# The transpose of the convolved x: four TensorE transposes a step, or VectorE 32x32 squares placed by DMA through memory

## What is computed

```
gate, xBC, dt = split(h @ in_proj_w.T)            # 8192, 8192 + 2*8*128, 128
xBC = silu(causal_conv4(xBC) + conv_b)
x, B, C = split(xBC)                              # 128 heads of 64; 8 groups of B and C
scores = (C @ B.T) * tril(exp(cs_l - cs_s))       # per head, chunks of 128 tokens, states carried over
y = scores @ (x * dt) + x * D                     # x * dt with tokens down the partitions
yg = y * silu(gate)
out = rmsnorm_per_group(yg) * norm_w @ out_proj_w.T
```

## Time and profile before

| what | us |
|---|---|
| median of 3 executions (1624.51 to 1627.74) | 1625.1 |
| the profiled execution's own time | 1627.01 |
| its span in the trace | 1625.2 |
| PE busy | 1564.3 (96%) |
| DVE busy | 1228.0 (76%) |
| POOL busy | 1052.0 (65%) |
| ACT busy | 1002.3 (62%) |
| mean DMA rate | 81 GB/s |

### The profile page before, as it was taken

The page is one execution under the profiler, slowest core; times in us unless marked ns, Lnnn a source line. Parts: engine busy times, 40 slices in busy tenths (PEclk is TensorE's granted clock), DMA queues, the critical chain, the costliest instruction groups (busy, mean ns, idle before and its releaser), DMA issues. The chain is left out here.

```text
span 1625.2 us, 25474 instructions
## 1 busy us (share of the span) xinstructions
PE 1564.3 (96%) x8296; PEld 1226.0 (75%) x8296; DVE 1228.0 (76%) x1689; ACT 1002.3 (62%) x2122; POOL 1052.0 (65%) x790
## 2 busy tenths in 40 slices
PE   6979999999999999999999999999999999999979
PEld 4657777777777777777777777777777777777757
DVE  6688877787778877887688877887688877887565
ACT  4357765666666665666666665666666665666431
POOL 2017874788757874788657874787657874787620
PEclk9899999999999999999999999999999999999989
DMA  3033321323222221222212321223222221322011
GB/s 118 1 103 103 107 91 59 92 91 92 78 72 92 92 92 59 91 92 92 78 72 92 92 91 59 92 92 92 78 75 88 92 92 59 98 86 84 20 40 53
DMA packets 73658, 131.65 MB, mean 81 GB/s; under 512 B 10944, under 2 KB 10944, under 8 KB 73280
## 3 DMA queue, kind: packets, MB, share of 16 engines
q1 hardware_dynamic: 73536, 130.09, 24.3%
HBM read 127.44 MB, written 2.62 MB: 80 GB/s over the span
## 5 line engine op out<-in xcount | busy, mean ns | idle before, releaser
L892 DVE SCALAR_TENSOR_TENSOR mx_acc<-bank,mx_cw,mx_acc 128x510 f32<-128x510 f32 (+2 forms) x480 | 358.3, 746 | 160.8 <-ACT mx_acc L877 149.5
L159 PE MATMUL bank<-h_hi,mx_w_hi 128*128 128x512 f32 x1152 | 465.6, 404 | 4.4 <-DVE mx_acc L892 2.3
L161 PE MATMUL bank<-h_hi,mx_w_lo 128*128 128x512 f32 x1152 | 453.1, 393 | 0.0
L160 PE MATMUL bank<-h_lo,mx_w_hi 128*128 128x512 f32 x1152 | 450.2, 391 | 0.0
L1108 ACT ACTIVATE mx_mix<-mx_csb,mx_gncs 128x256 f32<-128x256 f32 x512 | 218.9, 499 | 284.3 <-PE bank L1478 281.3
L1033 POOL TENSOR_TENSOR mx_y<-mx_y,mx_sg 128x512 f32<-128x512 f32 x128 | 338.4, 2644 | 59.7 <-DVE mx_y L1280 51.7
L839 POOL TENSOR_TENSOR mx_w_lo<-mx_w_raw,mx_w_hi 128x512 fp32r<-128x512 f32 x144 | 187.4, 1302 | 111.0 <-ACT mx_w_hi L834 111.0
L161 PEld LDWEIGHTS bank<-h_hi,mx_w_lo 128*128 128x128 f32 x1152 | 216.9, 188 | 48.5
L159 PEld LDWEIGHTS bank<-h_hi,mx_w_hi 128*128 128x128 f32 x1152 | 217.3, 189 | 47.8 <-issue 6.5
L160 PEld LDWEIGHTS bank<-h_lo,mx_w_hi 128*128 128x128 f32 x1152 | 217.7, 189 | 41.5
L1262 DVE TENSOR_TENSOR mx_mix<-mx_mix,mx_cbt 128x1536 f32<-128x1536 f32 x128 | 224.5, 1754 | 0.0
(11 more groups left out here) (163 smaller groups left out, 2203.7 us busy)
## 6 DMA issues: line engine op xcount, KB each, us to landing
mx_csb<-cs_rows SPq DMA_DIRECT2D x128, 512.0 KB, 4.0
mx_w_raw<-in_w_in SPq DMA_DIRECT2D x144, 256.0 KB, 4.0
mx_wo_raw<-in_w_out SPq DMA_DIRECT2D x64, 256.0 KB, 4.2
res<-in_x SPq DMA_DIRECT2D x8, 256.0 KB, 5.0
f_base_raw<-in_base_wt SPq DMA_DIRECT2D x2, 1024.0 KB, 6.1
out<-res SPq DMA_DIRECT2D x8, 256.0 KB, 2.0
f_a_raw<-in_lora_a SPq DMA_DIRECT2D x2, 256.0 KB, 3.8
f_lb_raw<-in_lora_b SPq DMA_DIRECT2D x2, 256.0 KB, 6.2
```

What stands on the lines that cost most here:

```text
L159: nc.tensor.matmul(out, w_hi, x_hi, start=first, stop=False)
L160: nc.tensor.matmul(out, w_hi, x_lo, start=False, stop=False)
L161: return nc.tensor.matmul(out, w_lo, x_hi, start=False, stop=last)
L892: self.nc.vector.scalar_tensor_tensor(dst, src[:, :, 0:SEQ - k], self.cw[:, c, TAPS - 1 - k:TAPS - k], dst, ALU.mult, ALU.add).then_inc(s[ ...
```

## The change

TensorE no longer transposes x. After `silu_conv` of unit `st + 4`, VectorE transposes that unit in 32x32 squares (`turn_squares`) into the slot of `th` whose tanh it has just used, laid out so that the squares of one 128x128 block lie row by row. SyncE (`move_x`) writes the slot to `x_dram` in memory and waits for that write, then loads it back with four DMAs, one for each 32 partitions of `xt`, in runs of 128 elements (512 bytes); all four count on `x_in`. `scale_x` reads `xt` instead of T_BANK and stands behind the taps of the step, `silu_conv` ahead of `silu_gate`, `turn_squares` of the next step's x behind `silu_gate`. `gdt` is laid out anew and made by four instructions a group instead of one. The copy `gncs` is gone: ScalarE reads the whole `ncs`. `square` writes into the gate's slot `sg` (the buffer `sq` is gone), and `tanh_gate` waits for the sums that read it. T_BANK, now S_BANK, holds the sums of squares alone. SyncE's groups are written out, not looped.

```diff
+            def move_x(g, st):
+                i, u = st % 2, st + 4
+                sp.wait_ge(s["turned"], 1 + STEPS * g + st + 1)
+                if not (first(g) and st < 2):
+                    x_moved(sp, *((g, st - 2) if st >= 2 else (g - 1, st + STEPS - 2)))
+                sp.dma_start(x_dram[i, :, :], th[:, u % 2, :]).then_inc(x_out[i], 16)
+                step_slot_freed(sp, s["xd"], g, st)
+                sp.wait_ge(x_out[i], 16 * (XT * g + st // 2 + 1))
+                for q in range(P // SQ):
+                    src = x_dram[i, :, q * P:(q + 1) * P].rearrange("(i r) e -> r i e", r=SQ)
+                    sp.dma_start(xt[q * SQ:(q + 1) * SQ, i, :, :, :].rearrange("r i t c -> r i (t c)"),
+                                 src).then_inc(x_in[i], 16)
...
                     if st == 10 and more:
                         ip.load_constants(sp, g + 1)
+                    move_x(g, st)
...
             def tanh_conv(g, u):
...
+                if u >= 6:
+                    x_moved(act, g, u - 6)
...
             def tanh_gate(g, st):
                 act.wait_ge(s["gate"], 1 + STEPS * g + st + 1)
-                act.wait_ge(s["yg"], 1 + STEPS * g + max(st - 1, 0))
+                if st >= 4:
+                    act.wait_ge(s["ssum"], 1 + SUMS * g + st - 3)
...
-                nc.scalar.activation(ssum[:, i, :] if st < 2 else sq[:, i, :], y[:, st, :],
+                nc.scalar.activation(ssum[:, i, :] if st < 2 else sg[:, i, :], y[:, st, :],
...
+            def turn_squares(g, st):
+
+                u = st + 4
+                dve.wait_ge(s["conv"], 1 + UNITS * g + u + 1)
+                nc.vector.transpose(th[:, u % 2, :].rearrange("p (q t c) -> p t q c", t=2 * HB, c=SQ),
+                                    acc[:, u % 4, :, :].rearrange("p b t -> p (b t)")).then_inc(s["turned"], 1)
+
             def scale_x(g, st):
...
-                dve.wait_ge(s["xt"], 1 + STEPS * g + st + 1)
+                x_moved(dve, g, st)
                 dve.wait_ge(s["y"], 1 + STEPS * g + max(st - 1, 0))
                 nc.vector.tensor_tensor(
-                    xd[:, i, :, :, :], T_BANK[:, :].rearrange("p (t h c) -> p t h c", h=2, c=HD),
-                    gdt[:, 4 * hf:4 * hf + 4, 2 * j:2 * j + 2].unsqueeze(3).to_broadcast([P, 4, 2, HD]),
-                    ALU.mult).then_inc(s["xd"], 1)
+                    xd[:, i, :, :, :].rearrange("p t h (i c) -> p (h i) t c", c=SQ), xt[:, i, :, :, :],
+                    gdt[:, hf, 2 * j:2 * j + 2, :, :].rearrange("p h i t -> p (h i) t").unsqueeze(3)
+                    .to_broadcast([P, P // SQ, 2 * HB, SQ]), ALU.mult).then_inc(s["xd"], 1)
...
             def steps(g, more):
                 for st in range(STEPS):
                     if st >= 1:
                         skip_y(g, st - 1)
                     make_mix(g, st)
-                    scale_x(g, st)
...
                     if here or more:
                         ip.taps(dve, gn, un)
-                    silu_gate(g, st)
+                    scale_x(g, st)
                     if here or more:
                         silu_conv(gn, un)
+                    silu_gate(g, st)
+                    if here:
+                        turn_squares(g, st + 1)
...
-            def transpose_x(g, st):
-                pe.wait_ge(s["conv"], 1 + UNITS * g + st + 5)
-                if st == 0:
-                    pe.wait_ge(s["ms"], 1 + g)
-                pe.wait_ge(s["xd"], 1 + STEPS * g + st)
-                for t in range(2 * HB):
-                    last = nc.tensor.transpose(T_BANK[:, t * P:(t + 1) * P],
-                                               acc[:, st % 4, t // 2, t % 2 * CH:(t % 2 + 1) * CH], m.ident[:, :])
-                last.then_inc(s["xt"], 1)
...
             def sum_over_channels(g, hf):
                 pe.wait_ge(s["ssum"], 1 + SUMS * g + SUMS - 1 + hf)
-                pe.wait_ge(s["xd"], 1 + STEPS * g + STEPS)
+                pe.wait_ge(s["ms"], 1 + g)
...
             def steps(g, more):
                 for st in range(STEPS):
-                    transpose_x(g, st)
```

More of the change, by code:

```diff
@@ L53 @@
 PAIR = SEQ + CH
+SQ = 32
+CONSTS = 7
 NE, RANK = 8, 16
@@ L800, in __init__ @@
         self.s = semaphores(nc, ctx, "mx", [
-            "const_in", "nw_in", "const", "proj", "gate", "xt", "y", "cb", "out", "ss",
+            "const_in", "nw_in", "const", "proj", "gate", "turned", "y", "cb", "out", "ss",
             "evac", "th", "tg", "decay", "sq", "yhi", "whi", "wohi", "gcopy", "root",
@@ L907, in mixer_phase @@
         wo_in = [ctx.enter_context(nc.semaphore(f"mx_wo_in{i}")) for i in range(2)]
+        x_out, x_in = ([ctx.enter_context(nc.semaphore(f"mx_x_{n}{i}")) for i in range(2)] for n in ("out", "in"))
         cs_in = [ctx.enter_context(nc.semaphore(f"mx_cs_in{i}")) for i in range(2)]
@@ L942, in step_slot_freed @@
                 eng.wait_ge(sem, 1 + STEPS * g + st - 1)
[L944 to L948, removed]
         def groups_in_turn(steps, tail):
@@ L1005, in group @@
                         ip.load_constants(sp, g + 1)
+                    move_x(g, st)
                 if more:
                     load_late(g + 1)
-            loop_groups(sp, group)
+            for g in range(NG):
+                group(g, g + 1 < NG)
         @block.gpsimd
@@ L1096, in tanh_conv @@
                 act.wait_ge(s["conv"], 1 + UNITS * g + max(u - 1, 0))
+                if u >= 6:
+                    x_moved(act, g, u - 6)
+                elif u < 2 and not first(g):
+                    x_moved(act, g - 1, STEPS - 2 + u)
                 nc.scalar.activation(th[:, u % 2, :], acc[:, u % 4, :, :].rearrange("p b t -> p (b t)"),
@@ L1123, in tanh_gate @@
                 act.wait_ge(s["gate"], 1 + STEPS * g + st + 1)
-                act.wait_ge(s["yg"], 1 + STEPS * g + max(st - 1, 0))
+                if st >= 4:
+                    act.wait_ge(s["ssum"], 1 + SUMS * g + st - 3)
+                elif st >= 2:
+                    act.wait_ge(s["yg"], 1 + STEPS * g + st - 1)
+                elif not first(g):
+                    act.wait_ge(s["ssum"], 1 + SUMS * g - 1 + st)
                 nc.scalar.activation(sg[:, st % 2, :], G_BANK[:, :], ACT.Tanh, scale=0.5).then_inc(s["tg"], 1)
@@ L1328, in head_constants @@
                 nc.vector.tensor_scalar(dh[:, :], d_raw[:, :], 0.5, None, ALU.mult).then_inc(s["const"], 1)
-                nc.vector.tensor_scalar(gdt[:, :, :], m.dtt[:, :, bass.ds(g * GH, GH)], 0.5, None,
-                                        ALU.mult).then_inc(s["const"], 1)
-                dve.wait_ge(s["const"], 1 + 5 * g + 5)
-            decay_constants(0)
+                for hf in range(2):
+                    for i in range(2):
+                        nc.vector.tensor_scalar(
+                            gdt[:, hf, :, i, :], m.dtt[:, 4 * hf:4 * hf + 4, g * GH:(g + 1) * GH].rearrange(
+                                "p t h -> p h t"), 0.5, None, ALU.mult).then_inc(s["const"], 1)
+                dve.wait_ge(s["const"], 1 + CONSTS * g + CONSTS)
             head_constants(0)
@@ L1344, in _ @@
             silu_conv(0, 4)
+            turn_squares(0, 0)
             def steps(g, more):
@@ L1385, in tail @@
                     silu_conv(g + 1, 4)
+                    turn_squares(g + 1, 0)
                 else:
@@ L1422, in _ @@
         def _(pe):
-            start_at_one(pe, [s["gate"], s["xt"], s["y"], s["cb"], s["ss"]])
+            start_at_one(pe, [s["gate"], s["y"], s["cb"], s["ss"]])
             start_after_quad(pe, [s["out"]])
@@ L1555, in program @@
 def program(nc, x, w_in, w_dt, conv_w, conv_b, dt_bias, d_skip, norm_w, w_out, base_wt, router_wt, lora_a, lora_b,
-            ncs_dram, out):
+            ncs_dram, x_dram, out):
     m = Chip()
@@ L1604 @@
     out = nc.dram_tensor("out", (TOK, HID), F32, kind="ExternalOutput").ap()
-    program(nc, ncs_dram=ncs_dram, out=out, **aps)
+    x_dram = nc.dram_tensor("x_squares", (2, P, HALF), F32, kind="Internal").ap()
+    program(nc, ncs_dram=ncs_dram, x_dram=x_dram, out=out, **aps)
     r = run_bass_kernel_spmd(nc, [{f"in_{k}": v for k, v in arrays.items()}], core_ids=[0])
```

45 lines of the change are left out of this document (20 added, 25 removed).

## The result

The changed kernel takes **1678.0 us** (median of 4, 1674.21 to 1682.2) against 1626.1 us for the kernel before beside it: a ratio of 1.032, 95% interval 1.0293 to 1.0347. It is slower by 52 us, where 30 us less were forecast, and lies outside the range.

What follows compares the result with a forecast made beforehand. The prediction took TensorE's own work to bound the kernel. It summed -52.5 - 19.4 + 30.4 + 11.9 = -29.6 us, giving 1595.5 us against the median, with a range from 1578 to 1658 us.

Steps and rivals of the forecast that it cites:

- What bounds the kernel: TensorE's own work sets the pace, with a matmul in flight for 96% of the span; VectorE next with 76%.
- Removed, 52.5 us, and a steady step of 9.87 us: 128 TensorE transposes at 0.41 us each go, 52.5 us less; a steady step falls from 10.28 to 9.87 us.
- The transpose, 0.75 us: Assumed time of VectorE's `turn_squares` in each step, with bounds of 0.69 and 1.6 us.
- The way through memory: Write, four loads and their issues between `turn_squares` and `scale_x`: 6.15 us, between 5.5 and 8.0.
- The loop through memory: Once-a-step loop of `turn_squares`, write, loads, `scale_x`, `silu_conv`, `silu_gate`: 9.1 us, hidden under the 9.87 us step.
- the limit of 6.91: Longest time in us from `turn_squares` through memory to `scale_x` that stays hidden in a steady step.
- Rival 1: The loop through memory becomes the bound, making the kernel slower, at 1658 us; chance 0.23.
- At nothing I cost: Items priced at zero: VectorE's 128 transposes' busy time, extra `gdt` instructions, squares into `sg`, SyncE's issues, added traffic.
- Rival 3: VectorE's transpose is dear, or its two-operand SBUF reads collide with GpSimd: 1613 to 1639 us; chance 0.12.
- The groups' starts, 30.4 us for the idle: At 8 groups' starts TensorE idles 3.8 us at `mix_tokens`, as memory time can't be hidden: +30.4 us.
- the wait of 19.4 us: TensorE's waits at the transposes for `silu_conv`, in 16 places, go with the instruction: -19.4 us.
- The clock, 11.9 us: TensorE's clock drops after the idle at 7 groups' starts, 1.7 us of work lost each: +11.9 us.

Runs made afterwards that it cites:

- experiment 9: The changed kernel with `silu_gate` back ahead of `silu_conv` and the two adds behind `make_mix` of the next step, `split_wo` unmoved: 1615.2 us.
- experiment 5: The changed kernel with GpSimd's sum of squares cut to one column of 512: 1647.8 us.
- Experiment 6: The kernel before, TensorE's transposes kept, with `scale_x` behind the taps and `silu_conv` ahead of `silu_gate`: 1634.2 us.
- experiment 11: The changed kernel with only unit 6 projected in step 0, in TensorE's idle time at a group's start: 1672.6 us.
- the fill and the later load of `mx_wo_raw`: Unit 6 projected in step 0 and `mx_wo_raw` loaded behind x; added to experiment 9's kernel: 1597.2 us.

## Why the prediction was wrong, by its own steps

- *What bounds the kernel*: right for before, with TensorE at 96%.
- *Removed, 52.5 us, and a steady step of 9.87 us*: right in size. It shows as 9.9 us in the steps outside the loop, and in nearly all of them in experiment 9. Group 0 is an exception that the sum left out: its first seven steps took 8.1 or 8.2 us before, not 10.28, and 8.3 to 10.4 us after.
- *The transpose, 0.75 us*: 0.70. *The way through memory*: the write 2.0 us as taken, the load 1.9 us for 2.2, the issues 1.74 us for four. The 0.1 us for VectorE to wake has no row of its own, but in the 48 steps in which `scale_x` waited the whole way, waking included, took 5.3 to 7.7 us with a median of 5.9, for the 6.15 of the sum. The loop through memory mostly stays under the step as said; four of the 48 are over the limit of 6.91, and all of this cost some 11 us in steps 1 to 14. Rival 1 was not what happened in the main. The section of the Trainium skill that it cites ("DMA: Bandwidth & Descriptors", "Anatomy of one DMA") describes DMAs issued by GpSimd, while SyncE issues them here.
- **The step that failed** is in "At nothing I cost": "the 128 VectorE transposes' own busy time (VectorE is idle for 24% of the span, and the loop above counts them)". I had looked for the new instructions in one loop, the new one, and taken VectorE's idle share for slack. A second loop, which goes through GpSimd and ScalarE, was in the trace with 0.87 us to spare. `turn_squares` and the swap of `silu_gate` and `silu_conv` both went into it, and so did `silu_conv`'s longer time. I had listed the swap among the changes and priced only its sum in the memory loop, where the order makes no difference. Measured: 10.9 and 11.5 us for 9.87 in the steps that the loop binds, and 63 us between the changed kernel and experiment 9, where the loop is open.
- *Rival 3*, the collision with GpSimd, was right in kind: `silu_conv` +0.29 us and `scale_x` +0.29 us on the mean. I put it at 1613 to 1639 us in the memory loop; in the other loop it is at most 30 us by experiment 5.
- *The groups' starts, 30.4 us for the idle*: 3.24 us instead of 3.8 in the start shown below, but not for the reason given: `scale_x` there, as in six of the eight starts, begins when the taps end, with no wait for the DMA. It is `scale_x` behind the taps that makes TensorE idle. Experiment 6 has 0.77 us of that idle with no DMA in the way, and the 1.71 + 0.41 us that TensorE no longer spends ahead of it make it 2.9: the wait of 19.4 us that the sum removed came back at `mix_tokens`. I had said moving `scale_x` costs nothing, which holds for the steady step only.

```profile
856.67 2.31 DVE L894 SCALAR_TENSOR_TENSOR mx_acc<-bank,mx_cw,mx_acc 128x510 f32<-128x510 f32 x3 [1.64 <-ACT mx_acc L879]
858.89 0.80 DVE L1297 TENSOR_TENSOR mx_xd<-mx_xt,mx_gdt 128x512 f32<-128x512 f32 x1
```

- *The clock, 11.9 us*: it fell as said after the idle:

```profile
859.75 1.12 PE L1492 MATMUL bank<-mx_mix,mx_xd 128*64 128x256 f32 x4 [3.24 <-DVE mx_xd L1297]
...
863.96 0.63 PE L161 MATMUL bank<-h_hi,mx_w_hi 128*128 128x512 f32 x1
```

The first matmuls behind the idle are slow already here (1.12 us for 0.65), and the granted clock is 0.50 until about 865.2. That is some 2.7 us, more than the 1.68 us I took. Over the span the mean clock is 0.974 for 0.989: some 25 us of full-clock work more (0.026 x 1676 less 0.011 x 1625), and experiment 11, which brings the clock back to 0.986, gains only 5 us by it and the filled idle together, since the loop hides the rest.

Left open: why group 0 lost some 8 us in its first eight steps, in experiment 9 as well; what makes the write land late in some steps; and what `square` into the gate's buffer and the new layout of `gdt` cost by themselves, which was not tried, nor were the fill and the later load of `mx_wo_raw` apart in the version with the loop open. Experiment 9 bounds the cost of the buffer and of `gdt`: its steady steps show nothing of them.

## What to carry to other kernels

Before an instruction is added to an engine that isn't the bound, follow every loop that passes through its place: from the instruction behind it, over the other engines' queues, back to it, and compare one turn with the step. An idle share of 24% says nothing of that slack, which here was 0.87 us of 10.28. An in-order queue makes links that no semaphore shows, such as `square` ahead of `tanh_conv`. And an independent instruction is best put where its engine waits anyway: the two adds behind `make_mix` instead of at the end of the step gave 40 us. `split_wo`, with two inputs in SBUF, lost by the same move, since it then started beside GpSimd's longest instruction: the place has to be free on both engines.

## What the runs showed of the hardware that I had not expected

- A VectorE instruction with two inputs in SBUF that starts while a GpSimd instruction is under way ends some 0.55 us behind it: `silu_conv` takes 0.68 us alone and up to 1.6 us, `split_wo` went from 0.74 to 1.65 us on the mean by its place alone (856.83 + 1.78 is 0.55 us behind 855.33 + 2.73). GpSimd takes longer too: the rounding remainder of y (L1052), started while `scale_x` ran, took 1.70 us, and 1.30 us in the kernel before.
- A transpose of 128x512 in f32, in squares of 32x32, takes 0.70 us on VectorE, no more than an ordinary instruction over as many elements.
- Four loads of 64 KB in runs of 512 bytes land in 1.9 us each on the median, as quickly as a write of 256 KB (2.0). The four issues take 1.74 us, but in 19 of the 128 steps of the changed kernel more, up to 2.9 us, in steps with a load of `mx_wo_raw` ahead and in others alike.
